# A stack of six layers on TensorE: the loop over the layers replaced by a program in sequence

## The reference, cut to what matters

```python
for i in range(DEPTH):          # DEPTH = 6
    x = attn_layer(shift_tokens(x), Wqkv[i], q_scale[i], k_scale[i], Wo[i]) + x
    x = ffn_layer(shift_tokens(x), ln_g[i], ln_b[i], W1[i], b1[i], W2[i], b2[i]) + x
```

## Time and profile before

| what | value |
|---|---|
| three runs | 4435.07, 4446.24, 4448.33 us (median 4446.24) |
| the profiled execution | 4434.56 us, span 4432.8 us |
| PE busy | 3666.4 us (83%) |
| DVE busy | 2661.7 us (60%) |
| ACT busy | 2213.7 us (50%) |
| POOL busy | 1684.8 us (38%) |
| local stack, from its first projection to its last turn | 611 to 2718 us |

### The profile page before, as it was taken

The page is one execution under the profiler, slowest core; times in us unless marked ns, Lnnn a source line. Parts: engine busy times, 40 slices in busy tenths (PEclk is TensorE's granted clock), DMA queues, the critical chain, the costliest instruction groups (busy, mean ns, idle before and its releaser), DMA issues. The chain is left out here.

```text
span 4432.8 us, 118638 instructions
## 1 busy us (share of the span) xinstructions
PE 3666.4 (83%) x48264; PEld 2787.7 (63%) x48456; DVE 2661.7 (60%) x4159; ACT 2213.7 (50%) x4350; POOL 1684.8 (38%) x1564
## 2 busy tenths in 40 slices
PE   4665759989979988988998996789999765667998
PEld 1223448858858867867876883577777751226555
DVE  5985567537727727736745754655655256894554
ACT  4443347647747746746755754344444314441222
POOL 2652047517607706725734742132222213560000
PEclk7988979999999999999999998788788777996999
DMA  0000011101101101101101100000000000001000
GB/s 14 0 0 17 1 46 33 39 20 34 45 15 31 34 19 41 33 24 35 34 29 30 32 21 4 7 6 7 6 6 7 3 12 0 0 0 58 0 0 9
DMA packets 56552, 83.19 MB, mean 19 GB/s; under 512 B 13146, under 2 KB 32628, under 8 KB 54900
## 3 DMA queue, kind: packets, MB, share of 16 engines
q1 hardware_dynamic: 56052, 75.99, 5.7%
HBM read 30.87 MB, written 1.05 MB: 7 GB/s over the span
## 5 line engine op out<-in xcount | busy, mean ns | idle before, releaser
L1850 POOL TENSOR_TENSOR local_rot<-local_term 128x512 f32<-128x512 f32 x384 | 478.7, 1267 | 643.9 <-DVE local_term L2168 643.9
L2168 DVE TENSOR_TENSOR local_term<-bank,local_table 128x512 f32<-128x512 f32 x768 | 485.2, 675 | 108.2 <-ACT local_sq L2056 99.7
L2091 ACT ACTIVATE local_attn<-bank 64x256 f32<-64x256 f32 x768 | 291.2, 379 | 340.3 <-PE bank L1947 333.5
L272 POOL TENSOR_TENSOR mamba_hc<-mamba_state,mamba_c_all 128x512 f32<-128x512 f32 x256 | 319.6, 1269 | 310.1 <-DVE mamba_state L451 304.8
L1856 POOL TENSOR_TENSOR local_rot<-local_rot,local_inv 128x512 f32<-128x512 f32 x384 | 392.8, 1044 | 93.9 <-ACT local_inv L2067 92.5
L1891 PE MATMUL bank<-local_w_layer,local_xs 128*128 128x256 f32 x1536 | 399.3, 405 | 27.5 <-issue 19.3
L1891 PEld LDWEIGHTS bank<-local_w_layer,local_xs 128*128 128x128 f32 x1536 | 286.9, 197 | 80.8 <-issue 31.2
L2229 DVE TENSOR_REDUCE local_most<-bank 128x8 f32<-128x512 f32 x192 | 132.8, 692 | 310.4 <-PE bank L1926 310.4
L1947 PE MATMUL bank<-local_pt,local_v_moved 64*128 64x64 f32 x3072 | 314.9, 283 | 0.0
L1947 PE MATMUL bank<-local_pt,local_v_at 64*128 64x64 f32 x3072 | 305.7, 277 | 0.0
L451 DVE TENSOR_TENSOR_SCAN mamba_state<-bank,mamba_dbu 128x512 f32<-128x512 f32 x256 | 300.3, 1222 | 0.0
(11 more groups left out here) (367 smaller groups left out, 8202.8 us busy)
## 6 DMA issues: line engine op xcount, KB each, us to landing
local_v_moved<-local_v_at SPq DMA_DIRECT2D x192, 192.0 KB, 2.4
local_w_layer<-a_w_layer_dram SPq DMA_DIRECT2D x6, 1536.0 KB, 7.1
local_v_moved<-local_v_at SPq DMA_DIRECT2D x192, 32.0 KB, 2.0
moe_w<-f_w_dram SPq DMA_DIRECT2D x3, 2048.0 KB, 16.1
local_w_o<-a_w_o_dram SPq DMA_DIRECT2D x12, 256.0 KB, 3.8
local_w_up<-a_w_up_dram SPq DMA_DIRECT2D x6, 341.0 KB, 4.4
moe_w<-f_w_dram SPq DMA_DIRECT2D x3, 576.0 KB, 4.8
delta_w_h<-g_w_qkv_dram SPq DMA_DIRECT2D x8, 192.0 KB, 2.2
```

What stands on the lines that cost most here:

```text
L272: ins = pool.tensor_tensor(hc[:, b, h, :], state[:, b, h, :], c_all[:, b, :], ALU.mult)
L1850: pool.tensor_tensor(rot[:, i % 2, :, f, :], here[:, :, f, :], there[:, :, 1 - f, :], ALU.add).then_inc(summed, 1)
L2091: ins = act.activation(tokens[ch, v, :, :].rearrange("p k (r q) -> p k r q", r=2), g.bank[6 + v][ch, :].rearrange("p (k r h q) -> p k r h ...
L2168: dve.tensor_tensor(term[:, which, b, :], g.bank[b][:, :], table[:, which, :, :].rearrange("p n c -> p (n c)"), ALU.mult).then_inc(roped, 1)
```

## The change

TensorE's loop over the layers becomes a loop of the program that writes the instructions: the body is emitted six times with `l` = 0 to 5 as a constant, and no instruction of TensorE branches or computes the value of a wait. The loops of the other four engines stay.

```diff
             for c in range(GROUPS):
                 turn(c, c)
-            with pe.Fori(0, LAYERS) as l:
+            for l in range(LAYERS):
                 pe.wait_ge(xs_ready, l * 8 + 4)
                 pe.wait_ge(pair_loaded, l * 16 + 16)
                 first = l * SLOTS
```

## The result

The changed kernel took 4415.45 us (median of 4 runs, 4414.04 to 4419.59) beside 4444.98 for the kernel before in the same comparison (4 runs, 4435.07 to 4448.33): ratio 0.9939, 95% interval 0.9921 to 0.9956. Four runs were few for this kernel. In a second comparison with 12 runs of the change and 35 of the kernel before, the change took 4417.3 and the kernel before 4435.02 (4416.58 to 4449.98): ratio 0.9961, interval 0.9946 to 0.9976. So the change makes the kernel about 0.4% or 17 us faster. Some 10 of the first comparison's 29 us lay in its four runs of the kernel before, whose median is 10 above that of the 35.

The account below looks back on a forecast made before the run. TensorE was taken to set the pace inside a layer, with late returns at layer edges; -4.72 - 1.2 + 3.0 = -2.9 us from the 4446.24 median gave 4443 us, range 4430 to 4451.

Parts of the forecast that it names:

- The edge now, and the removed branches: Between layers: TensorE returns 2.3 us sooner, ScalarE's return limits it; 4.72 + 1.2 = 5.9 us won over five edges.
- the 0.35 at the loop's entry: First projection's start behind ScalarE's last turn, 0.35 us when the loop was entered, assumed for every layer after the change.
- rival 3: At the edge ScalarE's return shortens too; at a full 1.0 us per edge 10.9 us faster, 4435; chance 0.08.
- Given back at the second projection: Behind each edge the second projection runs at the low clock after more idling: 0.6 us per edge, 3.0 lost.
- 5.9 - 3.0: Over five edges: 5.9 us won by removed branches, less 3.0 lost to the low clock at the second projection.
- Register instructions at 0: Waits in TensorE's steady slots: removing their register arithmetic wins 0, since the sequencer runs ahead; bound 21.3 us.
- the 0.5 that I left open: Unknown of 0.5 us either way for TensorE's waits that now need an instruction of their own.
- "Unchanged.": Matmuls, weight loads, semaphores, SyncE's transfers, the other four engines' loops and instruction traffic stay as they were; no term.
- Rival 4: Stage behind the stack: code cut worse into fetched pieces, 9 to 18 us more waits, 4449 to 4461; chance 0.15.
- Rival 5: Register instructions on TensorE's waits were on the path: up to 21.3 + 5.9 us faster, 4419; chance 0.05.
- Rival 6: At the edge an equal wait for fetched code replaces the branch's wait: no change, 4446; chance 0.10.
- the estimate of 0.5 us: Five branches between layers, at the skill's about 108 ns per compare-and-branch, would be worth 0.5 us.

Follow-up runs that it names:

- the hinted loop: Kernel before, TensorE's layer loop and register instructions kept, loop head fetched ahead by a hint at the body's top: 4425.15 us, ratio 0.9986.
- three kernels in sequence: Kernels with TensorE's and ScalarE's layer loops both written out, against the kernel before: ratio 0.9961 without spare activations at the edges.

## Why the prediction was wrong

**The edge now, and the removed branches.** Right. TensorE's gain is cut off by ScalarE's return, and the first square directly behind the table load shows it. The start behind the last turn is 0.05 us, not the 0.35 at the loop's entry, where the hinted loop, which keeps the register instructions, has 0.33 to 0.40; behind an edge it lies beside ScalarE's return and wins nothing. The first square gained 1.24 per edge where I had 0.94, as ScalarE's own return got shorter at three of the five edges (11.4 us of issue for five table loads in place of 12.9; 11.3 and 12.6 in the second profiles). That is a little of rival 3.

**Given back at the second projection.** Right in kind: 3.5 to 3.8 us, the low clock at every edge, behind 2.3 to 4.8 us of idle time. One step to it was wrong: the first projection was to run at the low clock, and it took 1.99 us at four of five edges. The first score gained 0.86 us per edge where 5.9 - 3.0 over five edges made 0.6.

**Register instructions at 0.** Right: score 3 to score 29 is 196.64 and 196.52 us before, 196.68 and 196.34 after, and the hinted loop has 196.53. Where nothing covers them, at the entry to layer 0, the first score comes 0.3 us sooner without them (14.15 and 13.83), within the 0.5 that I left open. The cover in the earlier trace rows is a microsecond of queued work (758.2 to 759.17), not the second that I wrote.

**"Unchanged."** This is the step that failed. I listed the rest of the layer as unchanged because its program is, and looked for the clock only at the edge. But the rest of the layer holds several low stretches, behind the first score, at the end of the slots and in the FFN, and its length goes with them: from the first score to the last turn it was 329.6 to 336.0 us in the kernels that have no spare matmuls. In the loop nearly every layer has the long form, near 351.6. With the first score 0.9 us sooner seven of ten have 348 to 349, and the mean is 2.4 us less. Beyond the edge's own 0.86 that makes 7.9 us over five layers. The forecast had 2.9 and nothing for the rest; the profiles have 4.3 for the edges, 7.9 for the rest of the layers, and 4.3 for layer 0.

How much of this is shown: that the gain comes from the edge's timing (0.9999, 0.9985 to 1.0012, when it is put back); that the layer does not follow the edge one for one (first score 12.56 and 14.29, both 348.1; 15.75, 350.2; 16.3, 351.6); and that a low stretch of the clock outside the edge costs 3.5 us a layer (0.9941 with the loop left alone). That the change wins its other 12 us by less time at the low clock has two supports: the 23.7 us less at 0.50, and the 6.9 us that are left of 16.5 when the end of the slots is filled in both kernels. Why an earlier edge puts fewer of the falls into the layer is open. Layer 0, which has no edge, had 344.2 and 343.9 us in the change, mostly because the clock held at the end of its slots (16.1 in place of 19.2 and 18.7). It had 349.4 and 347.3 in the two profiles of the loop, 347.0 with the hint, and 347.3 to 348.0 in three kernels in sequence; whether its gain is the change or where the clock stood when the stack began is open.

**The rivals.** Rival 4 did not come: the stage behind the stack, from its first matmul to its last, took 803.5 and 811.5 us in the kernel before and 803.3 and 803.5 in the change, with 54.1 us of issue beside 51.7. (Its near end was added up wrong: 4443 + 9 is 4452, not 4449.) Rival 5 is excluded by the steady slots. Rival 6 is refuted by the result, and so is the estimate of 0.5 us worked out from the Trainium skill's "Advanced Engine Details and Errata", Control Flow Timing. The Trainium skill's "TensorE: Matmul & The Clock Gate", Part 1: The HAM clock gate, says that the clock follows how busy TensorE has been of late; the fall after 2.7 idle us in slot 30, and its absence when those are filled, agree. I had cited the clock for one place and should have asked of every idle stretch in the layer.

**The comparison.** I set the sum against a median of three runs. The kernel before scatters from 4416.58 to 4449.98 over 35 runs, with a median of 4435.02. That is 11 of the 26 us between the forecast of 4443 and the 4417.3 measured; the other 15 are the gain that was 2.9 in the forecast and 17.7 by these medians. Over the 35 runs the time goes with the granted clock of the run (correlation -0.84).

## What to carry to other kernels

When a change moves the start of a phase, price not only the wait that it removes but every later place where TensorE sits idle for some us near a fall of its clock; the same program can be several us longer or shorter there. To win a few us at an edge, first close the idle gaps of TensorE with spare matmuls into a free bank: that won 26 to 29 us with no change to any loop. The engines' returns to the top of a long body can be read in the profile, and the one that is back last sets the edge. A hint on the loop's branch took 3.6 us of branch to 0.37 without writing the body out, though the runs show only a part of the gain for it.

## What the hardware showed unexpectedly

A taken branch out of a long body cost TensorE's sequencer 3.4 to 4.4 us in four profiles with the loop, and 0.36 to 0.38 with a hint at the top of the body. ScalarE's return cost 1.8 to 3.1 us of issue over the profiles that keep its loop. One low stretch of the clock (0.50 for 6.8 us) followed 2.7 us of idle time behind some 200 us of work at the high clock, and 12 matmuls of 0.23 us each, whose results nobody reads, prevented it in all six layers. In the kernels with a steady edge most layers gathered near a few lengths, 351.6, 348.1 and, with spare matmuls, 344.5 and 341.2 us: 1.7 us put in at every edge left 348.1 as it was. The change's own layers behind an edge lie between 348.1 and 351.5.
